# Gate/up weight tiles issued from ScalarE's DMA queue instead of SyncE's, in the recurrence stage of a two-layer block

## What is computed

```
def step(S, inp):                      # recurrence, over 512 time steps
    rt, kt, vt, dt = inp
    kv = kt[..., :, None] * vt[..., None, :]
    ot = jnp.einsum('bhk,bhkv->bhv', rt, S + bonus[None, :, :, None] * kv)
    S = dt[..., None] * S + kv
    return (S, ot)
...
gate_up = jnp.einsum('bsh,oh->bso', x, w_gu)      # gated MLP
gate, up = (gate_up[..., :I], gate_up[..., I:])   # I = 1408
h = jax.nn.silu(gate) * up
y = jnp.einsum('bsi,hi->bsh', h, w_down)
```

## Time and profile before

| | us |
|---|---|
| median of 3 runs | 1620.82 (1620.52 to 1621.89) |
| the profiled execution, its own time | 1624.38 |
| span of its trace | 1622.6 |
| `front` | 0 to 223 |
| recurrence and gate, first block | 223 to about 342 |
| second, third, fourth block | to about 456, 570 and 690 |
| linear attention | 690 to about 1240 |
| ReLU MLP | to the end |

### The profile page before, as it was taken

How to read it: one execution, slowest core, us unless ns; L and a number is a source line. 1 busy time by engine, 2 the same in 40 slices (tenths; PEclk the granted TensorE clock), 3 DMA queues, 4 the chain that set the end, 5 groups by cost and what they waited for, 6 DMA issues and landing times. The chain is left out here.

```text
span 1622.6 us, 20374 instructions
## 1 busy us (share of the span) xinstructions
PE 1575.8 (97%) x6768; PEld 1136.0 (70%) x6768; DVE 1101.2 (68%) x1584; ACT 438.6 (27%) x735; POOL 625.9 (39%) x482
## 2 busy tenths in 40 slices
PE   7999989999999999999999999999999999999998
PEld 3444456676677677678877777777776678888886
DVE  5787779787887899656457878787877655141422
ACT  2333341221221221322243333333332223131311
POOL 3686649736747568320032322323322331010101
PEclk9999999999999999999999999999999999999999
DMA  5534878767757765250200000000006424020010
GB/s 200 174 130 157 305 253 249 244 200 242 250 185 236 236 211 204 102 168 27 98 27 21 20 20 20 20 20 22 12 27 208 130 78 156 1 96 7 31 48 26
DMA packets 85539, 197.08 MB, mean 121 GB/s; under 512 B 7120, under 2 KB 28880, under 8 KB 77136
## 3 DMA queue, kind: packets, MB, share of 16 engines
q1 hardware_dynamic: 85312, 195.49, 36.3%
q10 hardware_dynamic: 144, 0.52, 0.1%
HBM read 154.05 MB, written 41.94 MB: 121 GB/s over the span
## 5 line engine op out<-in xcount | busy, mean ns | idle before, releaser
L2053 DVE SCALAR_TENSOR_TENSOR l_acc<-l_ps,l_inv,l_acc 128x512 f32<-128x512 f32 x240 | 165.9, 747 | 1.1 <-PE l_ps L773 0.4
L2563 DVE CAST g_x_part<-g_x 128x512 fp32r<-128x512 f32 x64 | 37.1, 580 | 190.2 <-ACT g_x L2615 190.2
L1925 POOL TENSOR_TENSOR relay<-l_expq,l_reluq 128x512 f32<-128x512 f32 x42 | 55.4, 1319 | 183.6 <-ACT l_expq L2198 183.6
L1095 POOL TENSOR_TENSOR r_rS<-r_S,first_r 128x512 f32<-128x512 f32 x64 | 94.1, 1474 | 74.3 <-DVE r_S L1199 74.3
L2496 POOL TENSOR_TENSOR relay<-relay 128x512 f32<-128x512 f32 x16 | 21.8, 1365 | 253.2 <-DVE relay L2544 253.2
L771 PE MATMUL r_ps<-relay_part,entry 128*128 128x512 f32 x256 | 104.6, 409 | 4.5 <-SPq L1034 2.9
L2029 DVE TENSOR_SCALAR l_expq<-l_ps,l_bq 128x512 f32<-128x512 f32 x64 | 48.0, 750 | 86.2 <-ACT l_reluq L2194 86.2
L771 PE MATMUL g_ps<-g_Wdn,g_x_part 128*128 128x512 f32 x256 | 103.1, 403 | 0.0
L1095 POOL TENSOR_TENSOR r_rS<-r_S,r_rT 128x512 f32<-128x512 f32 x64 | 96.7, 1511 | 15.4 <-DVE r_S L1199 15.4
L771 PE MATMUL l_ps<-l_M_part,l_sq_part 128*128 128x512 f32 x256 | 101.6, 397 | 0.8 <-DVE l_acc L2053 0.8
L772 PE MATMUL r_ps<-relay_part,entry 128*128 128x512 f32 x256 | 101.0, 395 | 0.0
(11 more groups left out here) (351 smaller groups left out, 4032.1 us busy)
## 6 DMA issues: line engine op xcount, KB each, us to landing
entry<-scratch_wgu SPq DMA_DIRECT2D x32, 1024.0 KB, 7.8
V<-scratch_v SPq DMA_DIRECT2D x96, 256.0 KB
relay<-scratch_x SPq DMA_DIRECT2D x15, 1024.0 KB, 7.4
r_w_part<-scratch_wgu SPq DMA_DIRECT2D x12, 1024.0 KB, 7.5
scratch_wgu<-f_halves SPq DMA_DIRECT2D x24, 384.0 KB, 4.0
relay<-scratch_v SPq DMA_DIRECT2D x32, 256.0 KB
scratch_x<-f_xT SPq DMA_DIRECT2D x4, 1024.0 KB, 6.7
relay<-in_Wq SPq DMA_DIRECT2D x16, 256.0 KB, 3.0
```

Source lines behind the costliest of these rows:

```text
L1095: nc.gpsimd.tensor_tensor(rS[u % RS][:, :], S[u % 2][:, 0:T], rT[u // DK][:, :], ALU.mult).then_inc(rS_ready.sem, 1)
L1925: nc.gpsimd.tensor_tensor(sq[i % N_SQ], expq[i % 2][:, :], reluq[i % 2][:, :], ALU.add).then_inc(sq_ready, 1)
L2053: last = nc.vector.scalar_tensor_tensor(acc[b][:, t, :], ps, scale, acc[b][:, t, :], ALU.mult, ALU.add)
L2563: nc.vector.tensor_copy(hi[:, :], x2[j % 2][:, :]).then_inc(x2_hi_ready.sem, 1)
```

## The change

Weight loads move from SP's program into ACT's. SP keeps only the very first one (tile 2 of the first block, ahead of everything else). On ACT each load stands right behind the SiLU of tile j, waits for the same product, and takes tile j+3 of the same block or, for j = 8, 9 and 10, tile 2, 0 or 1 of the next. In the last block the loads for j = 8 to 10 are left out. The number of loads and the bytes are the same (42 of 1 MB in this stage).

```diff
-            def load_weights(b, j):
-                if j >= NW:
-                    sp.wait_ge(*F.product(("gu", j - NW), b))
-                else:
-                    last = max(i for i in range(JT) if i % NW == j)
-                    sp.wait_ge(*F.product_before(("gu", last), b))
+            def load_weights(j):
                 sp.dma_start(w_part[j % NW][...], wgu[j * P:(j + 1) * P, :]).then_inc(part_loaded[j % NW].sem, 16)
...
-                    if u + 1 in following and following.index(u + 1) + NW < JT:
-                        load_weights(b, following.index(u + 1) + NW)
...
-                        load_weights(b + 1, 2)
-                    if u == 26 and not last:
-                        load_weights(b + 1, 0)
...
-                    if u == 29 and not last:
-                        load_weights(b + 1, 1)
...
-            load_weights(0, 2)
+            load_weights(2)
...
             sp.wait_ge(late, 10 * 16)
-            load_weights(0, NW)
...
+            def load_weights(b, j):          # in ACT's program
+                act.wait_ge(*F.product(("gu", j), b))
+                following = j + NW if j + NW < JT else j % NW
+                act.dma_start(w_part[j % NW][...],
+                              wgu[following * P:(following + 1) * P, :]).then_inc(part_loaded[j % NW].sem, 16)
...
                 for j in range(JT):
                     gate_silu(b, j)
+                    if j + NW < JT or not last:
+                        load_weights(b, j)
```

More of the change, by code:

```diff
@@ L1425, in gate_silu @@
                 nc.scalar.activation(silu_place(j), F.place(("gu", j))[0][:, :], ACT.Silu).then_inc(silu_gate_ready.sem, 1)
+            def load_weights(b, j):
+                act.wait_ge(*F.product(("gu", j), b))
+                following = j + NW if j + NW < JT else j % NW
+                act.dma_start(w_part[j % NW][:, :, :, :, :].bitcast(F32).rearrange("p h k s n -> p (h k s n)"),
+                              wgu[following * P:(following + 1) * P, :]).then_inc(part_loaded[j % NW].sem, 16)
             def high_hidden(b, j):
```

## The result

The changed kernel takes 1630.46 us (median of 20 runs, 1624.03 to 1633.13). The kernel before, timed beside it, takes 1622.83 us (20 runs, 1618.08 to 1629.76). The ratio is 1.0036, with a 95% interval of 1.0024 to 1.0047. So the change costs about 6 us, where -0.9 us had been forecast.

A forecast was written before the change was run, and what follows sets the result against it. TensorE was taken as the bound, with idle time to win almost only in the first block. Weight waits of 0.60 + 0.29 us would go, other terms nothing: 1620.82 - 0.9 = 1619.9 us, range 1617.8 to 1622.8.

The forecast's parts named there:

- What bounds the kernel: Recurrence stage: TensorE's idle time lies almost wholly in the first block; the relieved queue holds TensorE up for 0.9 us.
- The issue itself: Weight issues on ScalarE: each stands behind its SiLU and so goes about 0.6 us later.
- What stands behind it on ScalarE: High part or values' copy behind each weight issue: 0.33 us is covered, even the worst issue by 1.9 us; cost nothing.
- The landing: First block's weights in their own queue: land after 8.0 us, bounds 5.5 and 10.5; tiles 9 and 10 arrive in time.
- Who follows: First block, tiles 9 and 10: VectorE follows TensorE and the gain survives, 0.60 + 0.29 = 0.89 us, once.
- SyncE, freed: Value loads on SyncE go out up to some 5 us sooner but were never late; worth nothing.
- The next block's tiles: Tiles 2, 0 and 1 go out earlier, no longer behind the next x; TensorE never waited for them; worth nothing.
- The backlog rival: First-block landings stay at 14 to 15 us, later issue costs at most 1.8 us: 1622.6 us; chance 0.10.
- The slower rival: First-block weights land later from sharing with values, 5.1 us per step at tiles 4, 7, 10: 1636 us; chance 0.06.
- The faster rival: Sooner values speed up the recurrence; all TensorE waits in the first block, 3.6 us, could go: 1617.2 us; chance 0.04.
- What would show it: First-block landings 6 to 10 us, TensorE's weight wait gone, first block about 1 us shorter, next two unchanged within 0.2 us.

The follow-up runs named there:

- e1: Changed kernel, but the next block's tiles 2, 0 and 1 issued by SyncE at their old places; 1622.56 us, ratio 1.0002 to the kernel before.
- e13: e1 with the next x issued by ScalarE behind SiLU 10; 1624.35 us, ratio 1.0002 to the kernel before.
- v_before: Kernel before, with values stored a second time so that a value load has 16 outer rows instead of 8; 1641.10 us, ratio 1.0108.
- v_after: Changed kernel with the same second copy of the values as v_before; 1640.62 us, ratio 1.0109 to the kernel before.
- e6: Changed kernel, with the next x issued by ScalarE behind SiLU 10, ahead of tile 1, instead of by SyncE; 1625.05 us, ratio 1.0013.
- e7: Changed kernel, with only the next block's tile 2 back at SyncE's old place; 1627.41 us, ratio 1.0024 to the kernel before.
- e10: Changed kernel, with the early next-block tiles in the first block only, later blocks by SyncE at old places; 1627.89 us, ratio 1.0034.
- e11: Changed kernel, with ScalarE's high part of the next x moved behind squares(1) and y_silu(1); 1625.34 us, ratio 1.0024.
- e3: Kernel before, all loads on SyncE, but the next block's tiles issued right when gu 8, 9 and 10 are done; 1633.88 us, ratio 1.0067.
- e9_again: Repeat of e9, run beside a repeat of e1 on the same chip; 1624.16 us, ratio 1.0002 to the kernel before.
- after_again: The changed kernel run and profiled once more, nothing else changed; 1628.87 us, ratio 1.0042 to the kernel before.
- e9: Changed kernel, with the next block's tiles by SyncE at old places in the first block, early by ScalarE in later ones; 1625.20 us, ratio 1.0016.

## Why the prediction was wrong

**What bounds the kernel.** Right: TensorE's idle time lies in the first block, and the third block kept its length (114.02 us before and after). The second did not, by 4.30 us, as a late end of the first. The most that could be gained was read rightly. The base was low: the three runs of before gave 1620.82 us, the twenty 1622.83, so 2.0 us of the distance to the measured time are not the change's. What was left out is that a bound on the gain says nothing of the loss: everything that was just in time could become late.

**The issue itself.** 0.6 us later was wrong, harmlessly. The issue does not wait for the SiLU to end; both start at the product. ScalarE's timeline of after:

```profile
235.54 0.60 ACT L1412 ACTIVATE r_h<-r_ps 128x512 f32<-128x512 f32 x1 [3.50 <-PE r_ps L773]
235.55 0.33 ACTq L1417 DMA_DIRECT2D entry<-scratch_wgu  x1
```

The issue starts 0.01 us after the SiLU, and so do 37 of the 41; the other four start 0.46 to 1.23 us ahead of theirs, the first one (229.73) beside the table load that was to hold it up.

**What stands behind it on ScalarE.** Right: every weight issue took 0.33 to 0.35 us, and at tile 10, for instance, the high part starts after 0.75 us of waiting for VectorE, as in the earlier trace rows. What held up ScalarE later was not an issue but a load of another queue, that of x.

**The landing.** Right in kind, short in size. I took 8.0 us with 10.5 as the upper bound; the seven landings are 8.5 to 11.4, median 9.8. The weights pass the backlog. The prediction cites the Trainium skill, page "DMA: Bandwidth & Descriptors", section "Issuing engines are not separate DMA queues", for the rule that several issuing engines save only issuing time. This trace disagrees as far as landings go (14.6 to 9.8 us). It fits the rule's other half, that all run on the same 16 engines: VectorE's waits for values went from none to 7.9 us.

**Who follows.** "I expect it to move along" failed. With the weights' waits out and all else in place (e1, e13) TensorE waits for the reads instead, 3.3 to 5.9 us against 2.0, and the time stays. The row for it had stood in the group that I used for the gain: of TensorE's 3.6 us in the earlier trace rows the largest part was GpSimd's, fed by VectorE.

**"SyncE, freed ... They were never late. Worth: nothing."** This step failed. It took 18.5 us from issue to use as room, without a row that says how much of them the transfer needs. (The figure was also misread: the value used at 320.86 is the first of the two, issued at 302.32. And it is not the shortest, since the value issued at 234.36 was used 17.8 us later.) Near tile 9 the values had 19 to 21 us before, and VectorE didn't wait. In after one of them took 23.4 us, and VectorE waited 7.9 us in all. The other half of the step, that values go out sooner, was wrong as well: two near tile 9 went out 3.4 and 2.2 us later, behind a load that took 5.72 us to issue. "Values leave half of the engines' time free" was the premise. The pair v_before and v_after fits the reading that the free half was on engines that these loads don't use. What the late values cost in the median is open: e1, which has them, can't be told from before.

**"The next block's tiles ... TensorE never waited for them. Worth: nothing."** This is the step that decided the sign. The statement about TensorE is true, and it answers the wrong question. "No longer queue behind the next x" was read as harmless, but in after they were issued ahead of x. SyncE, held in long value issues, let x go out 5.9 us behind the product instead of right at it, and x took 15.7 us to land instead of 12.5. x had a reader with work behind it in an order written by hand: `high_x`, and behind it `squares(1)` and `y_silu(1)`, which vacate places for TensorE. The trace of before held what was needed: x was issued at 300.35, landed at 312.8 and was read by `high_x` at 315.12, so it had 2.3 us in hand. It had no row in the prediction. In after ScalarE waited 6.7 us for it, and TensorE 4.3 us for `y_silu`. e6 takes back some 4 of the 6 us by moving x alone; e7, e10 and e11 agree in their traces, and e3 shows that it takes no second queue.

**The rivals.** The backlog rival is refuted by the landings. The slower rival had the right sign for the wrong reason: it made the weights late, at 1636. They weren't; the values and x were. The faster rival held that VectorE's pace hangs on the values, which is true, but in the direction that I had given no chance. The chance of 0.06 for slower was too small because I priced one way of being slower, by the load that was moved, and none by the loads that stood around it.

**What would show it.** Of the signs named, "VectorE or TensorE waits for a value or a weight load" is the one that came; and the second block, which I had said would keep its length within 0.2 us, did not.

## What to carry to other kernels

When loads are moved to another queue or to an earlier moment, list every other load under way at that time, with its issue, its landing and its first use, and the work that stands behind that use in its engine's order; the slack that counts is theirs. In this kernel an early load that nobody waited for was not free. A transfer that shows about half of the engines' time may be running on half of the engines, as the pair with the new layout suggests, and then the rest of the time is no room in which others leave it alone.

## What the runs showed of the hardware that I had not expected

- In after, 37 of ScalarE's 41 weight issues started 0.01 us behind the start of the activation ahead of them, not at its end (235.54 and 235.55).
- An issue of SyncE can take many times its usual time. Value issues in the first block had a median of 0.62 us and at most 3.76 us before, and 0.71 us and at most 6.67 us after (to the `V` buffers; 7.92 us to the `relay` ones), though 1 MB loads had been taken out of that queue:

```profile
L984 SPq DMA_DIRECT2D V<-scratch_v x29: 596/713/6670, 230.2 to 347.1; - x29
L984 SPq DMA_DIRECT2D relay<-scratch_v x10: 609/1734/7917, 227.3 to 321.2; - x10
```

  In v_after, with the new layout, the 42 value issues in 243 to 370 took 0.54 to 0.62 us. What sets it was not tested further.
- TensorE's granted clock went to half (1.2 GHz) for 3.41 us at the end of an idle time of 4.0 us (at 287.7) and behind one of 2.8 us (at 349.2). Each of these waits so cost up to 1.7 us more than it was long. Idle times of 1.95 us in e3 and of 1.9 us in e9_again had the same behind them, one of 2.05 us in after_again had not. At the start of the stage the clock was at half for 6.83 us in before and after_again, for 3.41 us in e1, and not at all in after.
- The kernel before alone spreads from 1618 to 1631 us over its runs. A single trace may be off by more than the effect; the four kernels of this study with the same instructions in the first block (e1, e9 and their repetitions) start tile 9 between 62.8 and 67.6 us after tile 0.
